# Attention on four row groups of the array in float32r, its two loops reordered, and one DMA wait moved

## The reference, cut to what matters

```
x: 2 batches x 1024 tokens x 128 channels
mod = silu(c) @ wmod -> sa, ca, ga, sb, cb, gb
h = layernorm(x) * (1 + ca) + sa
q = h @ wq ; lat = h @ w_down (64) ; k = lat @ wk_up ; v = lat @ wv_up    # 16 heads of 8 channels
q, k = rope(q), rope(k)
scores = q k^T / sqrt(8), masked: key page <= query page (pages of 32 tokens)
x = x + ga * (softmax(scores) v) @ wo
h = layernorm(x) * (1 + cb) + sb
x = x + gb * more_ffn(h)      # 4 rounds, 4 experts, top 2, 128 -> 512 -> 128, gelu
```

## Time and profile before

| | us |
|---|---|
| median of three runs (769.58 to 771.03) | 771.0 |
| the profiled execution | 771.94 |
| its span, first to last instruction | 770.1 |
| attention's first matmul starts | 75.45 |
| its first scores start | 107.06 |
| project's first matmul starts | 341.27 |

### The profile page before, as it was taken

The page is one execution under the profiler, slowest core; times in us unless marked ns, Lnnn a source line. Parts: engine busy times, 40 slices in busy tenths (PEclk is TensorE's granted clock), DMA queues, the critical chain, the costliest instruction groups (busy, mean ns, idle before and its releaser), DMA issues.

```text
span 770.1 us, 12222 instructions
## 1 busy us (share of the span) xinstructions
PE 681.2 (88%) x3976; PEld 427.2 (55%) x4000; DVE 588.5 (76%) x1133; ACT 520.4 (68%) x905; POOL 183.8 (24%) x144
## 2 busy tenths in 40 slices
PE   3920988999699999987599999999999999999996
PEld 2410222333233333345478777787777877778885
DVE  5670987888588888229678898888988889888775
ACT  2530035677476777973488888888888888888984
POOL 0451016000000000000223343333433344322322
PEclk9965579999899999998799999999999999999998
DMA  9541041100101000000111110011100111101200
GB/s 237 150 139 65 0 117 40 43 21 25 46 2 44 24 20 4 3 1 1 66 45 55 56 56 28 29 56 56 55 34 24 54 56 57 54 2 55 69 15 28
DMA packets 17413, 37.20 MB, mean 48 GB/s; under 512 B 3305, under 2 KB 11241, under 8 KB 14533
## 3 DMA queue, kind: packets, MB, share of 16 engines
q1 hardware_dynamic: 16037, 34.65, 13.9%
q10 hardware_dynamic: 1312, 1.74, 0.9%
HBM read 31.86 MB, written 4.33 MB: 47 GB/s over the span
## 4 chain that ended last, share of the span: by engine, by line
PE 33%; DVE 12%; issue 5%; ACT 1%; POOL 0%; POOLq 0%; DVEq 0%
DVE gel_lo L1049 6%; PE y L952 6%; PE y L954 5%; PE y L953 5%; PE hid L943 5%; PE hid L942 5%; PE hid L941 5%; PE plog L963 2%; DVE part L1105 1%; ACT gel_hi L1017 1%; DVE at_least L1077 1%; PE pcw L972 1%; DVE cw L1096 0%; DVE cw L1094 0%; DVE dl L1084 0%
## 5 line engine op out<-in xcount | busy, mean ns | idle before, releaser
L1049 DVE TENSOR_TENSOR gel_lo<-gel,gel_hi 128x512 fp32r<-128x512 f32 x256 | 248.3, 1010 | 6.7 <-ACT gel_hi L1017 5.7
L588 DVE TENSOR_REDUCE mcol<-mx 128x1 f32<-128x512 f32 (+2 forms) x320 | 193.1, 635 | 61.7 <-PE mx L704 58.8
L562 ACT ACTIVATE probs<-st 128x512 f32<-128x512 f32 x288 | 155.7, 596 | 99.3 <-PE st L660 57.1
L1016 ACT ACTIVATE gel<-hid,b_sb 128x512 f32<-128x512 f32 x256 | 176.1, 688 | 38.5 <-PE hid L943 16.2
L1017 ACT ACTIVATE gel_hi<-hid,b_sb 128x512 fp32r<-128x512 f32 x256 | 174.7, 682 | 0.0
L1157 POOL TENSOR_TENSOR cur<-cur,part 128x512 f32<-128x512 f32 x64 | 106.4, 1663 | 250.8 <-DVE part L1105 250.8
L704 PE MATMUL mx<-ks,qs 125*128 125x512 bf16 (+3 forms) x384 | 120.8, 364 | 38.3 <-PEq L208 32.0
L952 PE MATMUL y<-gel_hi,w_hi 128*128 128x512 f32 x256 | 104.4, 408 | 0.4 <-DVE gel_lo L1049 0.2
L941 PE MATMUL hid<-cur_hi,w_hi 128*128 128x512 f32 x256 | 102.2, 399 | 0.4 <-DVE cur_lo L1123 0.4
L943 PE MATMUL hid<-cur_hi,w_lo 128*128 128x512 f32 x256 | 102.2, 399 | 0.0
L942 PE MATMUL hid<-cur_lo,w_hi 128*128 128x512 f32 x256 | 102.1, 399 | 0.0
(11 more groups left out here) (147 smaller groups left out, 521.9 us busy)
## 6 DMA issues: line engine op xcount, KB each, us to landing
cwb<-gate_rows SPq DMA_DIRECT2D x16, 1024.0 KB, 4.7
ks<-in_k_rows SPq DMA_DIRECT2D x3, 640.0 KB
qs<-in_q_rows SPq DMA_DIRECT2D x3, 616.0 KB
q_pieces<-pieces_q SPq DMA_DIRECT2D x4, 384.0 KB, 4.8
k_pieces<-pieces_k SPq DMA_DIRECT2D x4, 384.0 KB, 6.0
ks<-k_pieces SPq DMA_DIRECT2D x8, 192.0 KB
qs<-q_pieces SPq DMA_DIRECT2D x8, 192.0 KB
x_sb<-in_x SPq DMA_DIRECT2D x4, 256.0 KB, 5.2
```

Of the source, the lines that this page charges most:

```text
L562: nc.scalar.activation(probs[u % SLOTS][:, h, :], st[:, (HG * u + h) % ST_RING, :], ACT.Exp, scale=SCALE).then_inc(exp_done, 1)
L588: nc.vector.tensor_reduce(mcol[a % SLOTS][:, h, slot:slot + step * (len(blocks) - 1) + 1:step], mx[:, at % MX_RING, 0:len(blocks) * keys]. ...
L1016: nc.scalar.activation(gel[n % RING][:, :], hid[n % RING][:, :], ACT.Gelu_apprx_tanh, bias=bias)
L1049: nc.vector.tensor_tensor(gel_lo[n % RING][:, :], gel[n % RING][:, :], gel_hi[n % RING][:, :], ALU.subtract).then_inc(lo_ok, 1)
```

## The change

**Operands.** Each of q and k is cut into two float32r pieces in place of three bf16 ones, and three products in place of six are kept. A head's operand now has 24 rows of products, two rows for the maximum and four for the mask within a block of 128 tokens, padded to 32. Four heads stand under each other in one tile of 128 partitions (`ks`, `qs`: 128 x 1024, float32r), so head h of a group uses row group h of the array (partitions 32h to 32h+29). A score matmul that touches a block on the diagonal is split: 30 rows for that block, 26 (scores) or 24 (bins) for the others.

**Prep.** ACT makes the first piece and POOL the second; the second ACT copy and the second POOL subtraction are gone. SP writes three rows sets for each chunk and side (24 DMAs of 256 KB in place of 8 of 384 KB), and the constant rows go from DRAM to DRAM once (2 DMAs) in place of into each of the three slots (6 DMAs). A load of a group is 2 DMAs of 128 partitions in place of 12 of 24, 16 and 8 partitions. PE ends prep with nine matmuls whose result nobody reads (`BUSY_PREP`).

**The moved wait.** The wait for all pieces in DRAM stands in attention now, behind the loads of the ffn weights and of group 2. The wait for the constant rows stands ahead of the load of group 0.

**Bins.** Two heads share a bin: 20 bins of up to 2 x 512 columns for a group, in a ring of two pairs of banks. One DVE reduction reads both heads. The first 28 bins, before the first scores, are preceded by matmuls nobody reads: 5 each for four bins, then 2 (group 0) or 3 (group 1). The maxima are cut in two pieces on POOL, and four DMAs in place of one send them to `qs`.

**Units.** A group has ten units, eight of 512 columns and two of 256, each within one half of the queries, so `ov` is one bank. On PE the order in a unit k is: scores of heads 0 and 1, one bin pair, scores of head 2, one bin pair, scores of head 3, and then `weigh` of unit k-1, whole. `scores` of head h waits for the exponential three before it, as before. The lead of the bins is 14 units. There is no hardware loop any more.

```diff
-Q_PIECE = [0, 0, 0, 1, 1, 2]
-K_PIECE = [0, 1, 2, 0, 1, 0]
+Q_PIECE = [0, 0, 1]
+K_PIECE = [0, 1, 0]
...
+BUSY_PREP, BUSY_RISE, BUSY_FIRST, BUSY_LATER = 9, 5, 2, 0
...
-            m.ks = [ma.sb(f"ks{s}", [P, HG, T], BF16) for s in range(SLOTS)]
-            m.qs = [ma.sb(f"qs{s}", [P, HG, T], BF16) for s in range(SLOTS)]
+            m.ks = [ma.sb(f"ks{s}", [P, T], F32R) for s in range(SLOTS)]
+            m.qs = [ma.sb(f"qs{s}", [P, T], F32R) for s in range(SLOTS)]
...
 def load_group(sp, m, g, s):
-    for first, n in LOADS:
-        rows = slice(first * D, (first + n) * D)
-        sp.dma_start(m.ks[s][rows, :, :], ...
+    for dst, src in ((m.ks[s], m.kp), (m.qs[s], m.qp)):
+        sp.dma_start(dst[:, :].bitcast(F32), src[g].rearrange("h r t -> (h r) t")).then_inc(m.qk_in[s], 16)
...
-            sp.wait_ge(in_rows, 16 * SLOTS * 2)
-            sp.wait_ge(pieces_out, 16 * NCH * 2)
...
+            pe.wait_ge(h_ok, NCH)
+            for i in range(BUSY_PREP):
+                nc.tensor.matmul(turned[i % 2][:, :], m.ident[:, :], m.x[:, 0:TPC, :], start=True, stop=True)
...
-    ST_RING, MX_RING = 3, 3
+    ST_RING, PROBS, MX_RING = 3, 3, 2
...
+            load_group(sp, m, 2, 2)
+            sp.wait_ge(m.pieces_out, 16 * NCH * 2 * TERMS)
+            for g in range(GROUPS):
+                max_rows(g)
+                if g >= 1 and g + 2 < GROUPS:
+                    sp.wait_ge(st_done, HG * NU * g)
+                    load_group(sp, m, g + 2, (g + 2) % SLOTS)
...
+                for j, off, q0, nq in blocks:
+                    own = P if j // TPC == c else 0
+                    for rows, x, w in ((ROW_END, 0, own), (ROW_PAGE, own, nq - own)):
+                        if w:
+                            mm = nc.tensor.matmul(st[:, n % ST_RING, off + x:off + x + w],
+                                                  m.ks[s][r0:r0 + rows, j * P:(j + 1) * P],
+                                                  m.qs[s][r0:r0 + rows, ...], start=True, stop=True)
                 mm.then_inc(st_done, 1)
...
+            for k in range(STEPS):
+                scores(k, 0)
+                scores(k, 1)
+                bins(k + NU + LEAD, 0)
+                scores(k, 2)
+                bins(k + NU + LEAD, 1)
+                scores(k, 3)
+                if k >= 1:
+                    weigh(k - 1)
+            weigh(STEPS - 1)
```

More of the change, by code:

```diff
@@ L189, in prep @@
     ro = [l.sb(f"ro{s}", [P, 2, CH]) for s in "qk"]
[L190 to L191 removed]
+    pieces = m.pieces
     turned = [l.ps(f"turned{i}", [P, CH]) for i in range(2)]
@@ L651, in _, with scores @@
+            for g in range(GROUPS):
+                for n in range(NBINS):
+                    if n == 1 and g >= 1:
+                        merge(g - 1)
+                    if n == TURN_AFTER and g >= 1:
+                        keep_rows(g - 1)
+                    read_bin(g, n)
+            merge(GROUPS - 1)
+            keep_rows(GROUPS - 1)
         @block.tensor
         def _(pe):
-            def scores(i, a, u, h):
-                s, n = a % SLOTS, HG * (NU * gnum(i, a) + u) + h
+            def scores(k, h):
+                g, u = divmod(k, NU)
+                s, n, r0 = g % SLOTS, HG * k + h, HROWS * h
+                c, blocks = UNITS[u]
@@ L724, in body @@
-            def body(i, a):
-                for u in range(NU):
-                    nxt, side = following(i, a, u), part_at(i, a, u)
-                    for half in range(2):
-                        if exists(*nxt[:2]):
-                            scores(*nxt, 2 * half)
-                            scores(*nxt, 2 * half + 1)
-                        if exists(*side[:2]):
-                            part(*side, 2 * half)
-                        weigh(i, a, u, half)
-                        if exists(*side[:2]):
-                            part(*side, 2 * half + 1)
-                    if side[2] == 0 and exists(i, a + 1) and not exists(*side[:2]):
-                        turn_maxima(i, a + 1)
@@ L740, in _ @@
[L740 to L750 removed]
+                    own = P if k0 + keys == (t + 1) * P else 0
@@ new lines, in fill_bin @@
+                    for rows, y, w in ((ROW_MAX, 0, keys - own), (ROW_END, keys - own, own)):
+                        for i in range(PAIRS):
+                            r0 = HROWS * (2 * pair + i)
+                            if w:
+                                mm = nc.tensor.matmul(mx[:, at % MX_RING, i, x * keys + y:x * keys + y + w],
+                                                      m.qs[s][r0:r0 + rows, t * P:(t + 1) * P],
+                                                      m.ks[s][r0:r0 + rows, k0 + y:k0 + y + w], start=True, stop=True)
@@ new lines, in fill_bin, with keep_busy @@
+                mm.then_inc(bin_full, 1)
+            def keep_busy(g, n):
+                at = bin_at(g, n)
+                first = PAIRS * (NU + LEAD)
+                count = BUSY_RISE if at < 2 * PAIRS else BUSY_FIRST + g if NBINS * g + n < first else BUSY_LATER * (n % PAIRS == 0)
+                for i in range(count):
+                    nc.tensor.matmul(mx[:, at % MX_RING, i % 2, :], m.ks[g % SLOTS][:, 0:P], m.ks[g % SLOTS][:, 0:CH],
+                                     start=True, stop=True)
@@ new lines, in bins @@
+            def bins(unit, pair):
+                g, u = divmod(unit, NU)
+                if g < GROUPS:
+                    fill_bin(g, PAIRS * u + pair)
+                if pair == PAIRS - 1 and turn_due(unit) is not None:
+                    turn_maxima(turn_due(unit))
+            for unit in range(NU + LEAD):
+                for pair in range(PAIRS):
+                    bins(unit, pair)
+            for k in range(STEPS):
+                scores(k, 0)
[6 more added lines that the diff above has]
+                    weigh(k - 1)
```

450 lines of the change are left out of this document (174 added, 276 removed).

## The result

The changed kernel took 867.1 us (median of four runs, 852.49 to 873.64) against 770.3 before (median of four, 769.29 to 771.03), which is 12.6% more. Without its two slow runs (871.63 and 873.64) it is 11.3% more: ratio 1.113, 95% interval 1.102 to 1.125. The prediction, 721 with a range of 699 to 757, had the time fall, and it rose. What came is its rival D. The profiled execution is the shortest of the four, 852.49 us.

A forecast was written before the change was run, and what follows sets the result against it. It took idle DMAs to bound the start, DVE the first bins, PE the units with bins. Start 55.5, first bins 35, groups 199 and 2 put project at 291.5, 49.8 us less: 721 us, range 699 to 757.

The forecast's parts named there:

- rival D: Attention's units: TensorE falls to 1.2 GHz, a full unit 4.8 us, a group 45, all eight groups 885 total; chance 8%.
- Step 3: PE's work in a full unit: 2.5 us, with the two heads of a bin pair side by side on row groups.
- Step 4: Units: the loop through ACT's exponentials takes 2.4 us, just below PE's 2.5, so PE stays the bound.
- Step 1: Start of attention: first work at 55.5 us in place of 75, gain 19.5 us; ends 22 and 13, or 0.
- Step 2: First bins of attention: 35 us against 31.6 before, +3.4 us; ends 31 and 48.
- rival A: Units: row groups do not overlap, a full unit 3.0 us, a group 30, total 765; chance 13%.
- Step 5: A group of units: 24.9 us, eight of them 199; 0.5 us wait for maxima, no `issue` gap.
- The sum: Whole kernel: project starts at 291.5 us against 341.3, 49.8 us less, total 721.
- B: Start of attention: not gained in full, SP's issue blocks or group 0 lands late; start near 67, total 733; chance 15%.
- C: Units: PE drops off the path and DVE sets the pace while there are bins, total 699; chance 10%.
- E: Units: weight loads are not hidden where rows are the same, 8 us a group more, total 787; chance 2%.

The follow-up runs named there:

- e1: Changed kernel with every score matmul of the units over all 128 rows, bins still on row groups; 822.75 us.
- e7: Changed kernel with scores and bins both over all 128 rows; 779.08 us.
- e5: Changed kernel with the score and bin matmuls of all four heads on row group 0, 24 to 30 rows as before; 1011.58 us.
- e6: Changed kernel with score matmuls over 64 of 128 rows, bins still on row groups; 993.89 us.
- e3: Changed kernel with four added matmuls of 128 rows and 512 columns, read by nobody, in each unit that still has bins; 839.1 us.
- e4: Changed kernel with the wait for all pieces put back ahead of the end of prep, nothing else; 877.27 us.
- e2: Changed kernel with two added matmuls of 128 rows and 512 columns, read by nobody, in each unit that still has bins; 885.84 us.
- p1: Kernel before with only the order on PE changed: values of a unit in one piece behind all four heads' scores; 765.97 us, ratio 0.992.
- z2: Kernel before with loads of 8 partitions, the wait for the pieces moved into attention, and values in one piece; 755.67 us, ratio 0.981.
- p3: Kernel before with loads of 8 partitions and the wait for the pieces moved into attention, order on PE unchanged; 759.88 us, ratio 0.985.
- p2: Kernel before with only a group's loads changed: 12 DMAs of 8 partitions in place of 24, 16 and 8; 773.73 us, ratio 1.005.

## Why the prediction was wrong, point by point

- **The step that failed** is the clock under steps 3 and 4, and with it rival D's chance of 8%. All prices of a unit were taken at 1.00. The two reasons against D did not hold: "in the last units today PE waits as often and has 1.00" is true, but all those matmuls use 125 to 128 rows; and "the values still use all rows" is true of 1.87 of a unit's 4.06 us only, and with that the clock was 0.50. e1 and e7 show it from one side (128 rows: 1.00), e5 and e6 from the other (30 and 64 rows: 0.50 with PE busy all the time), e3 in between. Other values in the sums, or the other mask constant, are not the cause: e6 has both and 0.50, and e3 has neither and stretches of 1.00. That the rows decide in the units is shown so; why they do, inside the chip, is not. And rows are not all of it: the first bins of before use 125 rows and ran at 0.50 for 32 us, with PE busy 28.82 of them, and e1's first 28 us of scores over 128 rows ran at 0.50 as well. The Trainium skill (TensorE: Matmul & The Clock Gate, Part 1, What's actually happening) has the clock follow how busy the engine has been recently. If busy means what the profile's records count, these traces disagree: 350 of 350 us busy and 0.50.
- **Step 1** was right: 55.63 against 55.5, and SP was last. That it fits to 0.1 us is luck, as 55.5 was picked between 53.1 and 62, and its parts were less good: three issues of pieces took 1.9 to 3.2 us, so 0.6 to 1.1 each, not 0.4, and SP issued without a break from 42.83 to 54.98.
- **Step 2** was 7 us short, at a clock of 1.00 behind the first 7 us. The first four bins took 10.3 us (55.63 to 65.92), not 8, and the other 24 with the maxima 31.8 (to 97.68), not 27. DVE needs 1.22 us for 1024 columns, where the slope of smaller tiles gave 1.14. PE's timeline of the first bins and DVE's group (150 to 200 us) of the changed kernel:

```profile
55.67 2.47 PE L646 MATMUL mx<-ks 128*128 128x512 f32 x5 [4.58 <-PEq L201]
58.07 0.69 PE L635 MATMUL mx<-ks,qs 30*128 30x128 f32 x4
...
65.92 0.73 PE L646 MATMUL mx<-ks 128*128 128x512 f32 x2
```

```profile
L552 DVE TENSOR_REDUCE mcol<-mx 128x2 f32<-128x1024 f32 x18 | 21.2, 1221 | 12.6 <-PE mx L635 12.6
```

In e4, where the first bins ran at 0.50, the step was short by 25, beyond its upper end of 48.
- **Step 3**: the row groups do overlap, rival A is refuted by e3, and PE's work in a unit at full clock, without the added matmuls, is 2.26 us (forecast 2.5). Its values, with the change of array shape, take 1.00 (112.10 to 113.10; forecast 1.08).
- **Step 4** named the loop, and that loop became the bound. At 0.50 three of its pieces grow: values from 1.08 to 1.87, scores to exponential from 0.41 to 0.83, and scores of head 3 from 0.23 to 0.71, three times as long; exponential and release are as priced, 0.65. The sum is 4.06 us in place of 2.4. D's price, 4.8 a unit and 45 a group, had put scores and bins one after another, 2.8 us; they take 2.19 (200.40 to 202.59), 0.35 of it a wait. Measured is 40.7 a group.
- **Step 5**: no wait for `mrow`, no `issue` gap, as said.
- **The sum**: project starts 128.9 us later than forecast. 0.1 is the start, 7.0 the first bins, 121.7 the time from the first exponential on (322.7 against 201). So nearly all of the miss lies in the units, where the clock was 0.50. Behind project's first matmul it is 432.1 against 430.7 before.
- **Rivals** B, C and E did not come about; e7's 0.255 a matmul on the same rows speaks against E directly.

Both halves of the change's idea are seen by themselves: side by side at full clock e3 has PE's work of a unit below the forecast, and with all rows the clock is 1.00. No run had both without a price. With all rows a group takes 32.3 us in e7, more than before's 29.3: a float32r matmul over all rows is no cheaper than the bf16 one that holds all six products (0.234 against 0.22 us), and it is split more often.

## What to carry to other kernels

Before matmuls are packed into row groups because their contraction is short, ask what the clock will do: look in the trace for the granted clock of a stretch whose matmuls use as few rows. If there is none, price the plan at 0.50 and let one cheap run decide, the same kernel with its rows filled. Follow the loop through the other engines when you price a slower clock, not only PE's work. And take a large change apart: here 24.8 us (771.98 to 747.19) lay in four small parts of it that had nothing to do with its main idea.

## What the runs showed of the hardware that was not expected

- The granted clock stayed at 0.50 for 350 us and more of a PE that was busy without a gap, when its scores used 24 to 64 rows (e5, e6), and at 1.00 for 262.8 us with the same instructions over 128 rows (e1), after 28 us of such scores at 0.50.
- Tiles of different row counts did not run side by side. Between matmuls of the other size a pair of bins takes 0.43 us and a score of 128 rows 0.43 (e1); two pairs of bins and two scores of one tile size, six matmuls, take 0.68 (e3).
- Under the same order of matmuls, the first bins ran at 1.00 after 6.8 us in some executions (the changed kernel, e2, e3) and at 0.50 for 61 us and more in others (e1, e4, e6).
- The edge of the hardware loop cost PE a wait of 4.0 to 9.8 us once, between the first and second pass (4.0 in p1, 5.3 before, 8.5 in z2, 9.7 in p3, 9.8 in p2), and writing the loop out gave 8.5 us back.
